# A graph network's setup and norms: weights centred once, rows scaled at the eviction

## The reference

```python
# layer 0: hypergraph net with a residual
H  = (adj != 0); w = adj[0, :]
Dn = 1 / sum_e H[c, e] w[e];  Be = 1 / sum_c H[c, e]      # 0 where the sum is 0
conv(x, W, b) = Dn * (H @ (Be * (H.T @ (x @ W.T)))) + b
h = relu(conv(x, W1, b1))
h = (h - mean(h)) / sqrt(var(h) + 1e-5) * gamma + beta
x = layernorm(x + conv(h, W2, b2) + x)
# layer 1
agg = adj @ x / max(rowsum(adj), 1e-6)
x = layernorm(x + relu(concat([x, agg]) @ WL.T))
```

## Time and profile before

| | |
|---|---|
| median of 3 runs | 1110.5 us (1110.23 to 1110.59) |
| the profiled execution | 1110.66 us, of which the span of its instructions is 1108.6 us |
| TensorE busy | 1093.2 us (99%) |
| VectorE busy | 699.6 us (63%) |
| ScalarE busy | 314.9 us (28%) |
| GpSimd busy | 182.5 us (16%) |
| TensorE granted clock, mean | 0.998 |

### The profile page before, as it was taken

One profiled execution on the slowest core, in us unless ns is written; L12 is line 12 of the kernel. 1 busy time (PEld: TensorE's weight loads), 2 busy tenths in 40 slices (PEclk: granted clock), 3 DMA queues, 4 the chain that ended last, 5 costly groups with the idle time before them and its releaser, 6 DMA issues.

```text
span 1108.6 us, 18544 instructions
## 1 busy us (share of the span) xinstructions
PE 1093.2 (99%) x6112; PEld 899.0 (81%) x6112; DVE 699.6 (63%) x1846; ACT 314.9 (28%) x705; POOL 182.5 (16%) x256
## 2 busy tenths in 40 slices
PE   7999999999999999999999999999999999999997
PEld 6879697796978969688796887969789697887966
DVE  4665595665955768548685486754766646856326
ACT  4342302422124221333113331143301433024220
POOL 0222004120031202211031110401104020041000
PEclk9999999999999999999999999999999999999999
DMA  7017612067211572124611445115442075300001
GB/s 280 20 39 153 150 41 58 0 151 152 55 40 31 120 151 57 38 65 101 146 47 38 96 102 121 41 38 129 103 89 71 4 151 115 65 9 1 1 1 39
DMA packets 64599, 86.18 MB, mean 78 GB/s; under 512 B 9024, under 2 KB 54720, under 8 KB 64576
## 3 DMA queue, kind: packets, MB, share of 16 engines
q1 hardware_dynamic: 63520, 85.88, 33.6%
q10 hardware_dynamic: 1056, 0.00, 0.1%
...
## 4 chain that ended last, share of the span: by engine, by line
PE 94%; DVE 4%; DMA 1%; ACT 0%; issue 0%; ACTq 0%; DVEq 0%
PE bank L731 40%; PE bank L802 10%; PE bank L840 10%; PE bank L862 10%; PE bank L824 10%; PE bank L759 10%; PE bank L832 3%; PE bank L848 1%; DVE adjT L539 1%; DMA small<-in_L_gnn_gamma_dram 1%; DVE HT L544 1%; PE bank L768 1%; DVE o_f L676 0%; DVE xres L680 0%; ACT m_hi L389 0%
## 5 line engine op out<-in xcount | busy, mean ns | idle before, releaser
L731 PE MATMUL bank<-yv,adjT 128*128 128x257 f32 x1024 | 223.3, 380 | 0.0
L731 PEld LDWEIGHTS bank<-yv,adjT 128*128 128x128 f32 x1024 | 194.1, 190 | 31.3 <-issue 3.8
L394 ACT ACTIVATE small<-mv,small 128x1 f32<-128x1 f32 x192 | 56.6, 295 | 362.6 <-DVE mv L521 266.9
L759 PE MATMUL bank<-x_hi,H 128*128 128x258 f32 x512 | 122.8, 289 | 0.8 <-DVE m_lo L526 0.8
L731 PE MATMUL bank<-x_hi,H 128*128 128x256 f32 x512 | 122.6, 283 | 0.0
L731 PE MATMUL bank<-m_hi,HT 128*128 128x256 f32 x512 | 121.6, 281 | 0.0
L731 PE MATMUL bank<-x_lo,H 128*128 128x256 f32 x512 | 121.1, 281 | 0.0
L731 PE MATMUL bank<-m_lo,HT 128*128 128x256 f32 x512 | 120.9, 280 | 0.0
L526 DVE SCALAR_TENSOR_TENSOR m_lo<-bank,small,m_hi 128x256 fp32r<-128x256 f32 x128 | 61.1, 483 | 94.2 <-ACT m_hi L389 94.1
L824 PE MATMUL bank<-W1T,zT 128*128 128x512 f32 x256 | 120.4, 593 | 0.0
L840 PE MATMUL bank<-gW2T,xnT 128*128 128x256 f32 x512 | 119.8, 380 | 0.0
...
## 6 DMA issues: line engine op xcount, KB each, us to landing
...
```

Of the source, the lines that this page charges most:

```text
L394: nc.scalar.activation(std[:, i:i + 1], mv[:, which, i, 1:2], ACT.Sqrt, bias=eps_c)\
L731: last = mm(bank(stage, i)[:, 0:n_cols], lhsT, rhs, start=(k == 0 and part == 0), stop=(k == NT - 1 and part == parts - 1))
L759: last = mm(*args, start=(c == 0 and n == 0), stop=(c == NT - 1 and n == 1))
```

## The change

In the steady part: the mean is no longer subtracted from rows. `gW2T` is made from W2 times gamma with each output row's mean over DH removed, and each half of WL's rows has its mean removed, so that a row's mean drops out of the products. The factor 1/std is applied as Q and V leave PSUM. `centre("h")` and `centre("1")` go away on VectorE; the rows `xres` are normalised by ScalarE in eight passes behind the last V eviction. TH runs two steps behind P and Q three. In ScalarE's loop relu(s) stands behind the copy of TH(s-2), and zT's second chunk is taken at step 3 instead of 2. P is in fp32 before and after.

In the setup: the first loads are WL, x, adj's first rows, W1, more of adj, then W2 in two halves and beta and gamma as rows spread over all partitions; ScalarE's two loads are gone. VectorE centres WL, and TensorE's first work is WL's transposes. GpSimd multiplies W2 by beta and by gamma, ScalarE sums them (`sum_W2_beta` behind adjT's copies of c = 3, `centre_W2` behind those of c = 5), and W2's transposes and bW2's two small products stand among S1's last tiles. adj's transposes come one step later.

```diff
...
 SECOND_CHUNK = {0: (0, 1, 2), 1: (3, 4), 2: (5, 6), 3: (7,)}
-LAG_T = 3
-LAG_Q = 4
+LAG_T = 2
+LAG_Q = 3
 H_SLOTS = 4
...
-    W_FILLS = 3
-    W2_TURN, W1_TURN, WL_TURN = 0, 2, 4
-    BW2_BANK = 5
+    WL_TURN, W1_TURN, W2_TURN, BW2_TURN = 0, 2, 2 + NT, 3 + NT
     def adj_turn(c):
-        return c + min(c + 1, W_FILLS)
-    setup_fills = [0, 0, 0, 0, 0, 1, W_FILLS + NT, W_FILLS + NT]
-    setup_empties = [1, 1, 1, 1, 1, 1, W_FILLS + NT, W_FILLS + NT]
+        return 1 if c == 0 else 2 + c
+    setup_fills = [0, 0, 0, 0, 0, 0, 4 + NT, 3 + NT]
+    setup_empties = [1, 1, 1, 1, 1, 1, 4 + NT, 3 + NT]
...
-            sp.dma_start(W2n[:, :, :], W2.rearrange("(t p) d -> p t d", p=P)).then_inc(W2_loaded, 16)
+            sp.dma_start(WLn[:, :, :], WL.rearrange("(t p) d -> p t d", p=P)).then_inc(WL_loaded, 16)
             sp.dma_start(x_in[:, :, :], x[0, :, :].rearrange("(t p) d -> p t d", p=P)).then_inc(x_loaded, 16)
...
             sp.dma_start(W1n[:, :, :], W1.rearrange("(t p) d -> p t d", p=P)).then_inc(W1_loaded, 16)
-            sp.dma_start(WLn[:, :, :], WL.rearrange("(t p) d -> p t d", p=P)).then_inc(WL_loaded, 16)
             load_first_rows(1)
             load_first_rows(2)
+            for o in range(ND):
+                sp.dma_start(W2n[o][:, :], W2[o * P:(o + 1) * P, :]).then_inc(W2_loaded, 16)
+            sp.dma_start(beta_row[:, :], beta.partition_broadcast(P)).then_inc(rows_loaded, 16)
+            sp.dma_start(gamma_row[:, :], gamma.partition_broadcast(P)).then_inc(rows_loaded, 16)
             load_w(0)
...
+            pool.wait_ge(W2_loaded, 16 * ND)
+            pool.wait_ge(rows_loaded, 16 * 2)
+            for o in range(ND):
+                if o > 0:
+                    pool.wait_ge(W2_sum, o)
+                nc.gpsimd.tensor_tensor(W2b[:, :], W2n[o][:, :], beta_row[:, :], ALU.mult).then_inc(W2_product, 1)
+            for o in range(ND):
+                pool.wait_ge(W2_product, o + 1)
+                nc.gpsimd.tensor_tensor(W2n[o][:, :], W2n[o][:, :], gamma_row[:, :], ALU.mult).then_inc(W2_product, 1)
             pool.wait_ge(x_loaded, IN_0)
             pool.wait_ge(bias_loaded, 16 * 2)
-            pool.wait_ge(rDn_ready, 1)
+            pool.wait_ge(bW2_wide_done, ND)
+            pool.wait_ge(bank_full[TRANSPOSE_BANKS[0]], BW2_TURN + 1)
+            pool.wait_ge(HT_ready, NT)
...
-            act.dma_start(beta_c, beta.rearrange("(k p) -> p k", p=P), allow_slow_non_contiguous=True)\
-               .then_inc(rows_loaded, 16)
-            act.dma_start(gamma_c, gamma.rearrange("(k p) -> p k", p=P), allow_slow_non_contiguous=True)\
-               .then_inc(rows_loaded, 16)
             act.wait_ge(eps_ready, 1)
...
-            take_weights(W2_TURN, [W2T[:, 2 * k:2 * k + 2, :].rearrange("p k o -> p (k o)") for k in range(NH // 2)])
+            def sum_W2_beta():
+                for o in range(ND):
+                    act.wait_ge(W2_product, o + 1)
+                    nc.scalar.activation(W2b[:, :], W2b[:, :], ACT.Copy, accum_out=bW2_c[:, o:o + 1]).then_inc(W2_sum, 1)
+            def centre_W2():
+                for o in range(ND):
+                    act.wait_ge(W2_product, ND + o + 1)
+                    nc.scalar.activation(W2n[o][:, :], W2n[o][:, :], ACT.Copy, accum_out=gW2_sum[:, o:o + 1])\
+                      .then_inc(W2_sum, 1)
+                act.wait_ge(W2_sum, 2 * ND)
+                nc.scalar.activation(gW2_off, gW2_sum, ACT.Copy, scale=-1.0 / DH).then_inc(W2_off, 1)
+                act.wait_ge(W2_off, 1)
+                for o in range(ND):
+                    nc.scalar.activation(W2n[o][:, :], W2n[o][:, :], ACT.Identity, bias=gW2_off[:, o:o + 1])\
+                      .then_inc(W2_centred, 1)
+                act.wait_ge(ident_ready, 1)
+                for o in range(ND):
+                    nc.scalar.activation(bW2_wide[:, o, :], ident[:, :], ACT.Identity, scale=0.0,
+                                         bias=bW2_c[:, o:o + 1]).then_inc(bW2_wide_done, 1)
             split_first_x_hi()
+            take_weights(WL_TURN, [WLT[:, d, :] for d in range(ND)])
...
-            for c in range(NT - 1):
+            for c in range(NT):
                 take_adjT(c)
...
                     take_weights(W1_TURN, [W1T[:, d, :] for d in range(ND)])
-                if c == 1:
-                    take_weights(WL_TURN, [WLT[:, d, :] for d in range(ND)])
+                if c == 3:
+                    sum_W2_beta()
+                if c == 5:
+                    centre_W2()
             take_m_hi("S1", 0, 0, 0)
             take_m_hi("S1", 1, 0, 1)
-            take_adjT(NT - 1)
-            for e in range(2, NT):
+            take_weights(W2_TURN, [gW2T[:, 2 * k:2 * k + 2, :].rearrange("p k o -> p (k o)") for k in range(NH // 2)])
+            for e in range(2, NT - 1):
                 take_m_hi("S1", e, 0, e)
+            act.wait_ge(bank_full[TRANSPOSE_BANKS[0]], BW2_TURN + 1)
+            nc.scalar.activation(bW2_row[:, :], banks[TRANSPOSE_BANKS[0]][:, 0:D], ACT.Copy)\
+              .then_inc(bank_empty[TRANSPOSE_BANKS[0]], 1)
+            take_m_hi("S1", NT - 1, 0, NT - 1)
...
                 for s in range(NT + LAG_Q):
-                    if s < NT:
-                        act.wait_ge(*emptied("P", s, b))
-                        nc.scalar.activation(hrow[:, s % H_SLOTS, :], hrow[:, s % H_SLOTS, :], ACT.Relu)\
-                          .then_inc(relu_done, 1)
-                    if s == max(SECOND_CHUNK) - 1:
+                    if s == max(SECOND_CHUNK):
                         take_zT(1)
...
                     if s < NT:
+                        act.wait_ge(*emptied("P", s, b))
+                        nc.scalar.activation(hrow[:, s % H_SLOTS, :], hrow[:, s % H_SLOTS, :], ACT.Relu)\
+                          .then_inc(relu_done, 1)
                         root("h", 0, std_h, s, b)
...
                     act.wait_ge(*full("V", i, b))
-                    empties_bank(nc.scalar.activation(yv[:, i, 0:2 * D], bank("V", i)[:, :], ACT.Copy), "V", i)
+                    act.wait_ge(rstd_done["1"], b * NT + i + 1)
+                    empties_bank(nc.scalar.activation(yv[:, i, 0:2 * D], bank("V", i)[:, :], ACT.Identity,
+                                                      scale=rstd_1[:, i:i + 1]), "V", i)
                     if i + 2 < NT:
                         take_x1T(i + 2)
+                act.wait_ge(neg_mean_done, b + 1)
+                for i in range(NT):
+                    nc.scalar.activation(xres[:, i, :], xres[:, i, :], ACT.Identity, scale=rstd_1[:, i:i + 1],
+                                         bias=neg_mean_1[:, i:i + 1]).then_inc(normed["1"], 1)
                 for i in range(NT):
...
-            for n in range(BW2_BANK):
+            for n in range(TRANSPOSE_BANKS[0]):
                 nc.vector.memset(banks[n][:, 0:1], 0.0).then_inc(bank_empty[n], 1)
-            dve.wait_ge(rows_loaded, 16 * 2)
-            for k in range(NH):
-                nc.vector.tensor_copy(beta_wide[:, k, :], beta_c[:, k:k + 1].to_broadcast([P, P]))\
-                  .then_inc(beta_wide_done, 1)
-            def scale_W2T():
-                for n in range(NH // 2):
-                    dve.wait_ge(bank_empty[TRANSPOSE_BANKS[n]], W2_TURN + 1)
-                    for k in (2 * n, 2 * n + 1):
-                        nc.vector.tensor_scalar(gW2T[:, k, :], W2T[:, k, :], gamma_c[:, k:k + 1], None, ALU.mult)\
-                          .then_inc(W2T_scaled, 1)
+            halves = [WLn[:, o, side * D:(side + 1) * D] for o in range(ND) for side in range(2)]
+            dve.wait_ge(WL_loaded, 16)
+            for n, half in enumerate(halves):
+                nc.vector.bn_stats(stats[:, 0, n, :], half)
+            dve.drain()
+            for n, half in enumerate(halves):
+                nc.vector.bn_aggr(mv[:, 0, n, :], stats[:, 0, n, :])
+            dve.drain()
+            for n, half in enumerate(halves):
+                nc.vector.tensor_scalar(half, half, mv[:, 0, n, 0:1], None, ALU.subtract).then_inc(WL_centred, 1)
...
             split_first_x_lo(range(NT // 2, NT))
-            dve.wait_ge(bank_full[BW2_BANK], 1)
-            nc.vector.tensor_copy(bW2_row[:, :], banks[BW2_BANK][:, 0:D]).then_inc(bank_empty[BW2_BANK], 1)
             build_first_H(1)
-            scale_W2T()
+            build_first_H(2)
             for c in range(2, NT):
-                build_first_H(c)
+                if c + 1 < NT:
+                    build_first_H(c + 1)
                 build_HT_columns(c - 2)
...
                     sum_Dn(c - NT // 2, 0)
-            build_HT_columns(NT - 2)
             n_side = TRANSPOSE_BANKS[0]
             take_rBe(0, 0)
-            dve.wait_ge(bank_full[TRANSPOSE_BANKS[1]], adj_turn(NT - 1) + 1)
             for e in range(NT):
-                if e == 2:
-                    build_HT_columns(NT - 1)
                 if e + 1 < n_side:
...
                     take_rBe(e + 1, 0)
+                if e < 2:
```

(64 more changed lines are left out.)

24 lines of the change are left out of this document (15 added, 9 removed).

## The result

The changed kernel takes 1117.62 us (1117.46 to 1117.77, 4 runs) beside 1110.37 us (1109.59 to 1110.59, 4 runs) of the kernel before: ratio 1.0067, interval 1.0049 to 1.0084. It is slower, by 7.2 us (0.7%). The profiled execution took 1117.77 us, with a span of 1115.9.

The account below looks back on a forecast made before the run. TensorE, busy 99% of the span, was taken as the bound, so delaying the first P delays the end. Waits of 4.5 us plus 2.4 for the clock's fall gave 6.9 on 1110.66: 1117.4 us as median, range 1113.3 to 1119.9.

Parts of the forecast that it names:

- 45.55 (43.15 + 2.4): Setup, before P(0): m_lo of tile 2 at 43.15 behind ScalarE's W2 copies, plus 2.4 us for the clock's fall.
- Steady graphs 0: Steady part: only order moves, no product added or dropped, lateness hidden; 0 us change, 134.58 us per graph.
- Start 11.4, rise at 16.2, T(3) ends at 25.3: Setup: S1 starts at 11.4, the clock rises to full rate at 16.2, T(3) ends at 25.3.
- T(5) loses 0.85: Setup: W2's products and sums delay adjT(4)'s copies on ScalarE, so T(5), due at 29.0, loses 0.85 us.
- `centre_W2` 3.6 us, T(7) waits 2.85: Setup: `centre_W2` takes 3.6 us (3.0 to 4.2) in ScalarE's queue; TensorE idles 2.85 us before T(7).
- S1's tile 6 at 38.9: Setup: m_hi(0) now follows adjT(7), so S1's seventh tile starts at 38.9 after 2.0 us idle; shift +3.05.
- VectorE's path, 54.7: Setup's end: from m_lo(2) through Dn's sums to zT, 54.7 without the clock's fall; it sets P(0), +4.5 us.
- The clock falls again, +2.4: Setup, TensorE's gap: S1's tile 6 and W2's transposes at half rate, +2.4 us, bounds 0 and 3.0.
- the likeliest case: Setup: ScalarE's queue delays T(5) and T(7) and the clock falls: 1117.4 us (1115.6 to 1119.2), chance 0.48.
- Shared interface 0, with a bound of 2.5: Late sums of Dn: GpSimd's earlier residual overlaps VectorE's four sums; taken as 0 us, bound 2.5.
- The rival that priced it at 2.5: Late sums of Dn: the residual slows all four; up to 1119.9 us with the clock fallen, 1117.5 without; chance 0.10.
- The rival on the other side: Setup: W2 work fits ScalarE's gaps, `centre_W2` 1.0 us or less; P(0) at 50.9, 1111.2 us, chance 0.10.

Follow-up runs that it names:

- experiment 5: The kernel before with only the changed steady part, old setup and weights not centred: 1110.22 us beside 1110.18.
- Experiment 1: The changed kernel with 20 and 12 unread identity transposes filling TensorE's gap around T(7): 1115.22 us.
- experiments 4: The changed kernel with `centre_W2` behind m_hi of tile 1 instead of behind adjT's copies of c = 5: 1115.21 us.
- experiment 6: The changed kernel with 30 unread identity transposes ahead of WL's transposes and 4 behind them, keeping TensorE busy early: 1114.58 us.
- experiment 2: The changed kernel with GpSimd's first residual waiting for 1/Dn again, as before the change: 1116.52 us.
- experiment 11: The changed kernel with both the idle-work transposes in TensorE's gap and GpSimd's first residual waiting for 1/Dn: 1113.73 us.
- experiment 3: The changed kernel with two buffers for GpSimd's products of W2 and beta, so the second needn't wait for ScalarE's sum: 1117.75 us.

## Why the prediction was right

1117.4 was predicted and 1117.6 measured. The mechanism was right: ScalarE's queue holds up two groups of transposes, the clock falls in the gap, and the steady graphs change nothing. That the total came within 0.2 us was luck in part. VectorE reached m_lo of tile 2 at 44.92, where the prediction's terms give 45.55 (43.15 + 2.4), 0.6 sooner, and needed 0.8 longer from there; and the first rise, on which 1.1 us can hang, came at 17.0.

- *Steady graphs 0.* Right, by experiment 5 and by 134.58 us per graph. VectorE had 87.9 us of work in it and TensorE 134.58; taking 6.3 us from VectorE frees nobody.
- *Start 11.4, rise at 16.2, T(3) ends at 25.3.* S1 starts at 11.23, the rise is near 17.0, and the S1 step behind T(3) starts at 25.37. The sooner start and the later rise cancel. The rise had a range of 14.9 to 17.4 in the working; that it varies as much between runs of one start, the traces of the experiments showed.
- *T(5) loses 0.85.* It waits 0.25 on adjT, and the S1 step behind it 0.39 on H, which VectorE made late beside GpSimd: 0.64. The second cause was not in the working.
- *`centre_W2` 3.6 us, T(7) waits 2.85.* It took 3.9 (31.24 to 35.13). TensorE waited 2.0: the wait on H had made it later (T(6) ends at 33.66 instead of 33.05), and T(7) starts at 35.66 where 36.0 was predicted. The queue was read rightly, the wait was a little over-sized.
- *S1's tile 6 at 38.9.* 38.38, after a wait of 1.57 instead of 2.0. The terms up to here left it 0.5 us ahead of the prediction. From here the working has a small slip: by its own terms S2 would be at 44.3 (39.93 + 3.05 + 0.88 + 0.43) and not at 44.0, and P(0) at 54.6. VectorE's path, 54.7, stays the later one, so the sum stands.
- *The clock falls again, +2.4.* It did. Experiment 1 measured 2.4 by medians and 2.0 within the stage: 2.7 up to S2, less 0.7 that P then waits for zT. That it would fall was the likeliest case and not more: experiments 4 and 6 had gaps of 2.0 and 1.6 us in which it stayed.
- *Shared interface 0, with a bound of 2.5.* This term was mis-sized. The four late sums take 5.70 us instead of 4.90, so the chain to zT is 0.8 longer. The early residual costs 0.5 in experiment 2 and 1.2 in experiment 11, where TensorE arrives sooner (S2 to the first P; 1.1 and 1.5 by medians). The rival that priced it at 2.5 had the mechanism and a price too high: the sums grew by 4 to 28%, and not by the doubling of the earlier trace rows's `centre`. The Trainium skill (GPSIMD Engine Reference, Key points) has GpSimd contend for shared SBUF interfaces with VectorE's instructions of two SBUF inputs, and with those in a 2-port mode. The traces agree for the sums. The H and HT passes at 1.75 and 1.78, which read one tensor, grew as much (by 1.1 us); they need 0.69 us for 1024 columns where a sum needs 1.21, so they may be of the second kind, which no run here tells.
- *The rival on the other side* needed `centre_W2` within 1.0 us and fell with its 3.9.

Not settled: what sets the moment of the first rise, and why the clock falls in one gap of 2 us and not in another. What the later rise costs hangs on what follows: 2.5 us up to T(4) against a busy start, 2.0 of them kept at S1's tile 6 in experiment 6, nothing kept in experiment 3.
